# Attention and mixture-of-experts block: the last expert tiles by halves of 128 rows, sums of squares on TensorE, and matmuls that fill TensorE's pauses

## What is computed

```python
h = layernorm(x) * (1 + ca) + sa
x = x + ga * linear_attention(h)          # 16 heads of 8, causal running sums of k and k*v
h = layernorm(x) * (1 + cb) + sb
u = rmsnorm(h @ W_in.T, in_norm_w)        # 4096 tokens
idx = top_k(u @ Wr.T + expert_bias, 2)    # of 8 experts; gates: softmax over the two logits
oe = rmsnorm((silu(u @ Wg[e].T) * (u @ Wu[e].T)) @ Wd[e].T, enorm_w[e])      # 512 hidden features
x = x + gb * rmsnorm(sum of gate * oe, out_norm_w) @ W_out.T
```

## Time and profile before

| what | us |
|---|---|
| median of 3 runs | 413.69 (413.61 to 415.18) |
| the profiled execution, its own time | 414.08 |
| span of the profiled execution | 412.2 |
| TensorE busy | 354.4 (86%) |
| DVE busy | 323.8 (79%) |
| ScalarE busy | 291.9 (71%) |
| GpSimd busy | 236.5 (57%) |

### The profile page before, as it was taken

How to read it: one execution, slowest core, us unless ns; L and a number is a source line. 1 busy time by engine, 2 the same in 40 slices (tenths; PEclk the granted TensorE clock), 3 DMA queues, 4 the chain that set the end, 5 groups by cost and what they waited for, 6 DMA issues and landing times.

```text
span 412.2 us, 12923 instructions
## 1 busy us (share of the span) xinstructions
PE 354.4 (86%) x3757; PEld 307.9 (75%) x3758; DVE 323.8 (79%) x1037; ACT 291.9 (71%) x814; POOL 236.5 (57%) x211
## 2 busy tenths in 40 slices
PE   7899998999999999982069999999999999990464
PEld 4788886888888888861049889989899898980443
DVE  5568998899999999976928887878778877870696
ACT  5465776888888888546328878778778787773595
POOL 0665585688888888856341645454454445453441
PEclk9999998999999999995559999999999999997698
DMA  7899000000000000111423333333333333213833
GB/s 217 356 368 363 2 28 26 8 30 27 26 26 26 26 26 26 34 40 51 131 40 54 68 71 70 62 71 60 64 64 71 60 69 65 57 34 110 351 94 94
DMA packets 46563, 35.68 MB, mean 87 GB/s; under 512 B 36291, under 2 KB 42070, under 8 KB 45750
## 3 DMA queue, kind: packets, MB, share of 16 engines
q1 hardware_dynamic: 41862, 25.40, 21.9%
q0 software_dynamic: 4544, 9.39, 7.0%
q10 hardware_dynamic: 128, 0.53, 0.5%
HBM read 18.69 MB, written 13.47 MB: 78 GB/s over the span
## 4 chain that ended last, share of the span: by engine, by line
PE 70%; DVE 10%; ACT 6%; issue 5%; DMA 4%; POOL 1%; SPq 1%; DVEq 0%; ACTq 0%; POOLq 0%
PE bank L1474 12%; PE bank L1723 9%; PE bank L1724 8%; PE bank L1725 8%; PE bank L1738 4%; PE bank L1740 4%; PE bank L1554 4%; PE bank L1739 4%; PE bank L1497 3%; DVE prod L960 2%; ACT junk L835 2%; DVE wmaxs L1056 1%; PE bank L1561 1%; DMA cst<-consts 1%; PE bank L1581 1%
## 5 line engine op out<-in xcount | busy, mean ns | idle before, releaser
L559 POOL DMA_INDIRECT expert_rows<-late,to_place x78 | 79.2, 1015 | 85.9 <-DVE late L1333 73.3
L1723 PE MATMUL bank<-late,w_hi 128*128 128x256 f16 x312 | 86.4, 277 | 15.1 <-DMA late<-dispatched 13.7
L1724 PE MATMUL bank<-late,w_hi 128*128 128x256 f16 x312 | 86.4, 277 | 0.0
L1725 PE MATMUL bank<-late,w_lo 128*128 128x256 f16 x312 | 86.3, 276 | 0.0
L518 POOL TENSOR_TENSOR kv<-kv,v 128x1024 f32<-128x1024 f32 x32 | 67.7, 2134 | 32.0 <-ACT kv L686 32.0
L1319 DVE SCALAR_TENSOR_TENSOR kv<-bank,uscale,kv 128x512 f32<-128x512 f32 x78 | 58.5, 750 | 30.4 <-ACT kv L777 18.6
L536 POOL DMA_INDIRECT dispatched<-rows,pos x64 | 67.3, 1051 | 25.7 <-issue 18.2
L1474 PE MATMUL bank<-cst,kv 128*128 128x128 f32 x576 | 74.3, 279 | 0.0
L777 ACT ACTIVATE kv<-bank,descale 128x512 f32<-128x512 f32 x78 | 53.6, 687 | 24.0 <-PE bank L1725 20.1
L1474 PEld LDWEIGHTS bank<-cst,kv 128*128 128x128 f32 x576 | 68.9, 193 | 0.3 <-issue 0.2
L783 ACT ACTIVATE kv<-kv 128x512 f16<-128x512 f32 x78 | 48.8, 625 | 16.8 <-DVE kv L1319 12.3
(11 more groups left out here) (233 smaller groups left out, 733.2 us busy)
## 6 DMA issues: line engine op xcount, KB each, us to landing
late<-wguT SPq DMA_DIRECT2D x1, 4096.0 KB, 17.8
late<-expert_rows SPq DMA_DIRECT2D x1, 2064.0 KB, 10.9
gates_bc<-gate_rows SPq DMA_DIRECT2D x1, 2048.0 KB, 6.9
wd<-wdT SPq DMA_DIRECT2D x1, 2048.0 KB, 25.0
out<-kv SPq DMA_DIRECT2D x16, 128.0 KB, 1.8
late<-dispatched SPq DMA_TRANSPOSE x78
expert_rows<-late,to_place POOLq DMA_INDIRECT x78
late<-expert_rows SPq DMA_DIRECT2D x1, 1032.0 KB, 6.5
```

The lines of the kernel that those rows point to most:

```text
L559: pool.indirect_dma_start(ybuf, bass.IndirectOffsetOnAxis(ap=to_place[:, s, r:r + 1], axis=0), yt[:, s, r, :], None).then_inc(y_scat[s], 16)
L1723: mm(o, w_hi[:, w], hi, start=True, stop=False)
L1724: mm(o, w_hi[:, w], lo, start=False, stop=False)
L1725: last = mm(o, w_lo[:, w], hi, start=False, stop=True)
```

## The change

- **Late turn of the maxima.** The matmul with the row of maxima moves from the first to the second half of step 7; the one that spreads the power moves to the end of the step, into another bank, with waits of its own. `weight_power` stands behind the second products on DVE, `weight_scale` behind the counts.
- **Shifts of the norms** by one DVE operation in place of two (`norm_shift`).
- **Filling matmuls** (`keep_busy`, bf16, 512 columns, results unused): 5, 13, 3 and 12 in the drain, 24 behind the totals, 8 behind the wait for the scatters, 46 ahead of the last stage.
- **Loads of tiles** by one transposing DMA in place of two; SyncE loads its registers ahead of the wait for scatters and fillers. Columns of the weights are addressed in bytes (`columns_of`).
- **Last two tiles** in halves of 128 rows: a bank for each half, squares, scaling and scatter per half, and the first half's square of the last but one tile ahead of the high part of the last tile.
- **Last stage.** ScalarE squares the transposed rows in one instruction, TensorE sums them against a column of ones. The second load's roots come ahead of the first batch's work, the fourth load's one batch earlier.

```diff
         MAX_STEPS = range(SCALE_STEP - 4, SCALE_STEP)
-        MAX_ALL = CUM[1][:, THIRD * P:THIRD * P + 1]
+        MAX_ALL = FFN[:, L + NT * E:L + NT * E + 1]
...
+                if not again_turn(i):
+                    sp.wait_ge(filled, 16 * (E + 1))
+                    sp.wait_ge(scattered[0], 16 * NT * K * (B // 2))
+                    sp.wait_ge(scattered[1], 16 * NT * K * (B // 2))
...
-                for half in range(2):
-                    sp.dma_start(hT3[:, s, half], hbuf16[bass.ds(row, R), half * D:(half + 1) * D],
-                                 transpose=True).then_inc(slot_ld[s], 16)
+                sp.dma_start(hT3[:, s], hbuf16[bass.ds(row, R), 0:2 * D], transpose=True).then_inc(slot_ld[s], 16)
...
-                    if scale and cc == 1:
-                        if t == 0:
-                            pe.wait_ge(wmax_done, 1)
-                            mm(MAX_ROW, wmax[:], ident, start=True, stop=True)
-                        else:
-                            pe.wait_ge(wpow_done, 1)
-                            mm(MAX_ALL, ones[0:1, :], wpow_row[:], start=True, stop=True)
+                    if scale and t and cc == 1:
+                        pe.wait_ge(wmax_done, 1)
+                        mm(MAX_ROW, wmax[:], ident, start=True, stop=True)
...
+                if scale:
+                    pe.wait_ge(wpow_done, 1)
+                    pe.wait_ge(ohs_done, rte[0] + 1)
+                    mm(MAX_ALL, ones[0:1, :], wpow_row[:], start=True, stop=True).then_inc(wall_ps, 1)
+            def keep_busy(bank, n):
+                for _ in range(n):
+                    mm(bank[:].rearrange("p (a n) -> p a n", n=P), ones16[:],
+                       ones16[:].unsqueeze(1).to_broadcast([P, 4, P]), start=True, stop=True)
...
+            act.wait_ge(y_ps, TILES - 1)
+            last_square(LAST - 2, 0)
             high_part(TILES - 1, LAST - 1, TURNS - 1, 1)
+            last_square(LAST - 2, 1)
+            for r in range(RB):
+                act.wait_ge(last_y_ps, r + 1)
+                last_square(LAST - 1, r)
...
+            def squared(b, p, n):
+                act.wait_ge(mixT_ps, b + 1)
+                if again(n):
+                    act.wait_ge(sq_ps, b - 1)
+                nc.scalar.activation(mixsq[:, p, :], bk[p][:, 0:L], ACT.Square).then_inc(sq_done, 1)
+            def rms_out(b, p, n):
+                act.wait_ge(sq_ps, b + 1)
+                if again(n):
+                    act.wait_ge(rinv5_done, b - 1)
+                nc.scalar.activation(rms5[:, p, :], bk[4 + p][:, 0:NT], ACT.Sqrt, bias=eps_rms[:],
+                                     scale=1.0 / D).then_inc(rms5_done, 1)
...
+            with act.Fori(2, B // 4) as i:
+                for j in range(4):
+                    squared(*batch_of_turn(i, j))
+                    rms_out(*batch_of_turn(i, j - 1))
+                    turned(*batch_of_turn(i, j))
...
+            def sums_of_squares(b, p, n):
+                pe.wait_ge(sq_done, b + 1)
+                if again(n):
+                    pe.wait_ge(rms5_done, b - 1)
+                for t in range(NT):
+                    last = mm(bk[4 + p][:, t:t + 1], mixsq[:, p, t * P:(t + 1) * P], ones[:, 0:1], start=True, stop=True)
+                last.then_inc(sq_ps, 1)
...
             pe.wait_ge(wgb_done, 1)
+            pe.wait_ge(last_rows, 2)
+            keep_busy(CUM[0], 46)
             def turn_of_batches(i, batches=range(4)):
                 for j in batches:
                     stage_d(*batch_of_turn(i, j))
+                    sums_of_squares(*batch_of_turn(i, j - 1))
                     stage_e(*batch_of_turn(i, j - 1))
```

More of the change, by code:

```diff
@@ L264, in block_kernel @@
         yb = late[:, 0:B * NT * K * YW].rearrange("p (n k w) -> p n k w", k=K, w=YW)
-        half, mix, mixT = (prod[:].rearrange("p t s -> p (t s)")[:, i * 2 * L:(i + 1) * 2 * L].rearrange(
-            "p (j t d) -> p j t d", j=2, t=NT) for i in range(3))
+        half, mix, mixT, mixsq = (prod[:].rearrange("p t s -> p (t s)")[:, i * 2 * L:(i + 1) * 2 * L].rearrange(
+            "p (j t d) -> p j t d", j=2, t=NT) for i in range(4))
         ob = kv[:, 0].rearrange("p t s -> p (t s)")[:, 0:4 * L].rearrange("p (j t d) -> p j t d", j=4, t=NT)
-        mixT = mixT.rearrange("p j t d -> p j (t d)")
+        mixT, mixsq = (m.rearrange("p j t d -> p j (t d)") for m in (mixT, mixsq))
         rms4, rinv4, coef = (sb(n, [P, B * NT, K]) for n in ("rms4", "rinv4", "coef"))
-        ssq4 = sb("ssq4", [P, 2, NT])
         rms5 = sb("rms5", [P, 2, NT])
@@ L565, in _ @@
                     scatter_tile(s, n)
-            for s in range(LAST):
+            for s in range(LAST - 2):
                 scatter_tile(s, TURNS)
+            for s in range(LAST - 2, LAST):
+                for r in range(RB):
+                    pool.wait_ge(last_rows, RB * (s - LAST + 2) + r + 1)
+                    pool.indirect_dma_start(
+                        ybuf, bass.IndirectOffsetOnAxis(ap=to_place[:, s, r:r + 1], axis=0),
+                        yt[:, s, r, :], None).then_inc(y_scat[s], 16)
             def halve(b, p, n):
@@ L881, in norm_shift @@
                 dve.wait_ge(rs_done, b + 1)
-                for t in range(NT):
-                    last = nc.vector.tensor_scalar(nmr_[:, p, t:t + 1], mv_[:, p, t, 0:1], -1.0, rs_[:, p, t:t + 1],
-                                                   ALU.mult, ALU.mult)
-                last.then_inc(nm_done, 1)
+                nc.vector.scalar_tensor_tensor(nmr_[:, p, :], mv_[:, p, :, 0], -1.0, rs_[:, p, :], ALU.mult,
+                                               ALU.mult).then_inc(nm_done, 1)
             dve.wait_ge(x_first, 16)
@@ L1720, in gate_up, with down @@
                     o = (G, U)[part][h][:, c * R:(c + 1) * R]
-                    w = bass.ds(e * F + (part * E * F + (h * (FC // 2) + c) * P), P)
-                    mm(o, w_hi[:, w], hi, start=True, stop=False)
-                    mm(o, w_hi[:, w], lo, start=False, stop=False)
-                    last = mm(o, w_lo[:, w], hi, start=False, stop=True)
+                    wh, wl = (columns_of(w[:], e, F, part * E * F + (h * (FC // 2) + c) * P) for w in (w_hi, w_lo))
+                    mm(o, wh, hi, start=True, stop=False)
+                    mm(o, wh, lo, start=False, stop=False)
+                    last = mm(o, wl, hi, start=False, stop=True)
                 last.then_inc((g_ps, u3_ps)[part], 1)
-            def down(t, s, i, e):
+            def down(t, s, i, e, apart=False):
                 if s >= 2 or again_turn(i):
@@ L1755, in turn_of_tiles @@
                     if s:
-                        down(t - 1, s - 1, i, ex[s - 1])
+                        down(t - 1, s - 1, i, ex[s - 1], apart=last and s == LAST - 1)
                     elif not first:
```

125 lines of the change are left out of this document (80 added, 45 removed).

## The result

| | before | changed |
|---|---|---|
| median, us | 414.44 (413.61 to 416.49, 4 runs) | 448.20 (446.31 to 451.34, 4 runs) |
| ratio, 95% interval | | 1.081 (1.074 to 1.089) |
| profiled execution, span, us | 414.08, 412.2 | 448.59, 446.5 |

What follows compares the result with a forecast made beforehand. The prediction took TensorE's columns to bound the expert tiles, and chains of waits the edges. Its terms, -1.5 -0.3 -1.2 -0.7 -1.9 -0.5 +8.4 = +2.3, on 414.08 gave 416.4 us, range 410 to 421.

Steps and rivals of the forecast that it cites:

- Norms' shifts: In the steps, one DVE operation for two saves DVE 0.3 us a step: minus 0.3 us (0 to minus 1).
- Edge 5: The last stage, first mix to last output: 35.7 us against 27.7, plus 8.4 with slow pieces (5.2 to 11).
- The ring: Last stage: each mix waits for the mix before through TensorE and ScalarE, 2.1 us a batch (1.9 to 2.3).
- rival 3: The clock is lost in the last stage: 421 us if half of the rings are slow, 425 if all; chance 0.12.
- the early terms: The gains forecast ahead of the last stage, for shifts, maxima, drain, dispatch, ramp and last tiles: minus 6.1 us together.
- Edge 1: Step 7, with the maxima: the late matmul ends the step 1.8 us earlier; minus 1.5 us (0 to minus 3.5).
- Edge 2: The pipeline's drain: two router matmuls and a transpose leave half clock if fillers keep the clock; minus 1.2 us.
- Rival 4: Fillers in the way: the clock falls in the drain despite 5 fillers and the others overrun their gaps; 422 us, chance 0.05.
- Edge 3: Dispatch to first tile: earlier register load and one transpose for both halves; minus 0.7 us (0.4 to 1.6).
- The ramp: First tile: with fillers ahead, 2 us are slow in place of 5.5; minus 1.9 us (0 to minus 2.8).
- Edge 4: The last tiles: the last scatter goes at 374.66 and not 375.15; minus 0.5 us (0 to minus 0.6).
- Rival 1: The ring is no bound, last-stage batches keep to DVE's 1.35 us: 405.5 us in all, chance 0.17.

Runs made afterwards that it cites:

- e2: The kernel before with one edit, the norms' shifts as one DVE operation in place of two: 434.62 us, ratio 1.050.
- e1: The changed kernel with the two 128x1 operations back at the norms' shifts, nothing else: 425.36 us, ratio 1.030.
- e6: The kernel of e1 with 4 filling matmuls behind each batch's output matmuls in the last stage: 422.31 us, ratio 1.014.
- e10: The kernel of e5 with the row of maxima and the power at their old places: 410.22 us, ratio 0.985.
- e11: The kernel of e5 with every filling matmul left out: 421.23 us, ratio 1.016.
- e12: The kernel of e5 with two transposing transfers of 128 columns a tile in place of one of 256: executions from 409.36 to 421.25 us.
- e5: The kernel of e1 with the last stage reordered, sums and root of batch j-1 ahead of transposes and square of j: 407.30 us, ratio 0.980.
- e9: The kernel of e5, first norm's shift again one operation, its second tensor in PSUM: 405.18 us in one execution, 417.41 to 419.71 in three.
- e15: The kernel of e13 again, on one chip beside the kernel of e5: median 409.98 us, ratio 0.985.
- e13: The kernel of e5 with 6 and 4 fillers in TensorE's pauses at the last stage's start: 423.01 us on a slower chip, ratio 0.979.
- e3: The kernel before, its two 128x1 shift operations kept but each with two tensor operands: 438.15 to 453.57 us, ratio 1.065.
- e7: The changed kernel with the two 128x1 operations back at the first norm's shift only: 431.45 us in one execution.

## Why the prediction was wrong

- **Norms' shifts, forecast -0.3 (0 to -1): +20.8 by e2, +21.6 by e1** (first to last denominators). This is the step that failed: "One operation for two at the norms' shifts saves DVE 0.3 us a step; where TensorE bounds the step this is worth nothing". It counted instructions and took their price from the old form. It didn't ask which other engine works at that moment, and what the new operands are. The forecast rightly had TensorE as the bound of a step, but the 2 us hold up what DVE hands to TensorE, and TensorE waits 1.36 us a step for it. The trace before could have warned: the shift stands 0.10 us behind the start of GpSimd's 4.22 us. It couldn't have shown the wait.
- **Edge 5, forecast +8.4 (to +11): +17.4.** The ring is there, with 2.12 us at full clock for the forecast's 2.1 (bounds 1.9 and 2.3), and 1.89 to 2.06 in e6's first batches with full clock; idle time at the reciprocal is put down to ScalarE's root, as foretold. Its loop takes 2.2 to 2.4 since the address work of 0.25 us ahead of a mix, which I took as an upper bound, is paid in every batch. The rest is rival 3, the lost clock: I gave it 0.12, and it took 5.8 us (e6). "I add 0.4 for a few slow pieces" is the term that failed. Its price of 0.67 us a ring was near: 0.3 in the first batches, 0.6 in the loop (2.9 against 2.3 in e6). 414.1 with the early terms and this rival is 425, and e1, which has the whole change but the shifts, took 425.36. That it fits so well is luck in part: the early terms gave 7.8 us in e1 for the forecast's 5.8, and the start, which no edit touches, took 1.7 back. ScalarE was busy 15.45 of the stage's 45.05 us, a third and not two thirds; already the forecast's own 1.05 us in a ring of 2.1 is a half.
- **Edge 1, maxima, forecast -1.5:** the size came out (e1 -1.3 over two steps), the reason didn't. By e10 the late turn is worth 0.1; what I priced as a shorter chain was the clock, which falls in that pause in some executions and not in others.
- **Edge 2, drain, -1.2:** -1.5; the fillers fit, the clock was 1.00. e11 has it at 0.50 without them. Rival 4 didn't come (its sum is 422.6, not 422).
- **Edge 3:** total to first tile -1.1 for -0.7. One double transpose takes 1.2 us to issue, not 2.3: I took the wrong end of the bounds. The rule of the Trainium skill that stood beside it ("DMA: Bandwidth & Descriptors", Rules for kernel authors), to join small transfers, points the right way, and the trace agrees as to the issue: 1.2 us for two halves as for one. But the -1.6 that I had put beside it didn't come: issue to first tile fell by 0.64 us, and the register load out of the way gave 0.33. The 8 fillers end behind the landing, which I had named as a sign of being wrong; by e11 and e12 it costs tenths.
- **The ramp, -1.9:** -2.4 by e11 and e5 (164.19 and 161.74). The clock was full at the first tile. That is luck in part: in the profiles of e6, e9, e10, e12 and e15 the first tile still starts at half clock behind the same fillers, and the stretch takes 162.3 to 162.9 us.
- **Edge 4, -0.5:** can't be told. With the tiles of before the stretch is 163.93 to 165.28 us in three profiles, in e11, with the new ones and no fillers, 164.19.
- **Rival 1** (the ring is no bound) falls. Had TensorE and ScalarE had their operations in the order of e5, it would have been the case, and with the shifts mended the time 407: its sum said 405.5.
- The forecast looked at timing edges that it could price, and the larger part of the change's cost was in the one edit that it priced at nothing.

## What to carry to other kernels

When operations are merged, compare the forms and not the count: look up for each operand whether it is a tensor in SBUF, one in PSUM or a value per partition, and look in the timeline at what GpSimd does at that moment. Where an engine works on batch j and then j-1, follow one batch's result round through every queue: an order may close a ring that swapping two lines opens (e5, 18 us with the clock that it cost). A filler is worth most ahead of a stage of small matmuls, and in the first pauses of it, since a clock lost there can stay lost for the whole stage (e9, e11, e13 to e15). Where nothing is idle behind a filler, see whether it holds up the work itself.

## What the runs showed of the hardware

- A DVE operation with two tensors in SBUF, beside a GpSimd instruction that reads SBUF, ends when that one ends: 2.04 or 0.92 us for 0.16, and 2.11 us for a pair of 128x1 that takes 0.23 elsewhere in the step (e3).
- The other way round, GpSimd's indirect scatter seems to wait for DVE. The first scatter of a step takes 1.64 us in the kernel before (1.71 in the changed one, 1.42 in e7) and not 0.96 when DVE's w_lo operation (two tensors in SBUF) runs beside it, and ends 0.88 us after that one in the kernel before, in the changed one and in e7. GpSimd's timeline before, and then DVE's:

```profile
151.47 1.64 POOL L536 DMA_INDIRECT dispatched<-rows,pos  x1 [0.33 <-issue]
...
172.03 1.00 POOL L536 DMA_INDIRECT dispatched<-rows,pos  x1 [0.23 <-issue]
```

```profile
150.94 1.29 DVE L1069 SCALAR_TENSOR_TENSOR w_lo<-late,w_by,w_hi  x1
```

  At 172.03 no such operation runs, and it takes 1.00. The same page of the Trainium skill, "SBUF — State Buffer", Who interferes with whom, infers that writing descriptors doesn't wait for an operation that only reads through the shared pair; these rows speak against it. No run here changed this alone, so it isn't shown.
- A stage of small float32 matmuls at half clock kept TensorE busy 33.56 of 35 us, and the clock at 0.50 (e11). It isn't always so: in e10 and e12 TensorE was as busy at half clock, and the clock came back about halfway through the stage.
